# A decoder layer on one core: the last three token blocks in idle banks, chunks ahead of a down projection, and filling transposes

## The chip, the cores and the metric

The kernel runs on one core of one Trainium2 chip. The metric is the device time of one execution in microseconds (us), lower is better. TensorE, VectorE (DVE), ScalarE (ACT), GpSimd (POOL) and the DMA queue of SyncE (SP) each work through a queue of their own in order; semaphores order them against each other.

## The reference

The input `x` has 8 batches of 256 tokens with 512 features. Three residual layers follow each other, each with a layer norm behind it:

```python
x = _layernorm(x + _L0_attn_ref(x, Wi, Wf, Wg, w_norm, Wo))      # gated linear recurrence
x = _layernorm(x + _L0_xattn_ref(8, 256, 512, w, u, x, ctx_2048)) # WKV: two recurrences, a division
x = _layernorm(x + _L0_ffn_ref(x, w_gate_up, w_down))
```

The change touches the third one, a feed-forward layer with values rounded to whole multiples of a scale for each row:

```python
def _quant_dequant(v, axis):
    scale = jnp.max(jnp.abs(v), axis=axis, keepdims=True) / QMAX
    scale = jnp.maximum(scale, EPS)
    q = jnp.clip(jnp.round(v / scale), -QMAX, QMAX)
    return q * scale

xq = _ste(x, axis=-1)                      # _ste gives the value of _quant_dequant
gate_up = jnp.einsum('bsh,oh->bso', xq, _ste(w_gate_up, axis=-1))
gate, up = (gate_up[..., :I], gate_up[..., I:])        # I = 1408
h = jax.nn.silu(gate) * up
return jnp.einsum('bsi,oi->bso', _ste(h, axis=-1), _ste(w_down, axis=-1))
```

A token's hidden row of 1408 values has to be complete before its maximum, and so its scale, is known; only then can it be rounded and projected down.

## The kernel before

A batch of 256 tokens is two token blocks of 128; block `n = 2b + t` is block `t` of batch `b`, 0 to 15 in all. Each engine's program is an order written out by hand. A prologue handles the first batches and the weights; a loop over `iteration(b, par)` runs the feed-forward layer of batch `b` beside the WKV layer of batch `b + 1` and the recurrence of batch `b + 2`. Behind the loop stands a tail, again by hand: the feed-forward layer of batch 6 beside the WKV layer of batch 7 (there is no batch 8), and then the feed-forward layer of batch 7 alone. The whole change lies in the tail.

A token block goes through the feed-forward layer in these steps, named by their functions:

- `mlp_up(b, par, t, [c])`, PE: chunk `c` of the up projection. There are three chunks, of 512, 512 and 384 hidden columns; each is 8 matmuls, 4 for the gate and 4 for the up half, into one of two slots of `slot_ps` (two banks each), slot `(t + c) % 2`. PE may write a slot when VectorE or ACT has read what lay in it.
- `scale_products(b, t, [c])`, DVE: multiplies the gate half into `gate_buf` and the up half into `hid_buf(t)` by the scales of the weights' rows; the second of them frees the slot (`mlp_read`).
- `silu(b, par, t, [c])`, ACT, in place in `gate_buf`; `hidden(b, t, [c])`, POOL: the product of both, in place in `hid_buf(t)` (`hid_ready`).
- `hidden_max_row(b, t)`, DVE: the largest magnitude of the whole row. For block 15 it is taken in pieces: `hidden_max(b, t, c)` for each chunk and `hidden_max_last` over the three. `hidden_scale`, DVE: three one-column instructions to `hid_inv`.
- `round_hidden(n, t, part)`, ACT: rounds the row in two parts of 768 and 640 columns. `turn_hidden(n, t, part)`, PE: turns them by 6 and 5 transposes into a slot. `read_hidden(n, t, part)`, ACT: copies them into `hqT` (`hq_ready`).
- `mlp_down(n, t)`, PE: 11 matmuls of 512 columns into the first bank of slot `(t + 1) % 2`. `read_down`, DVE: reads and scales them into `z3` (`down_read`).
- `residual_3`, POOL, `layer_norm_3`, DVE, `rstd_3`, POOL (four one-column instructions), `normalise_3`, ACT: the residual and the layer norm; the store follows on SP. For blocks 14 and 15 VectorE does the residual and the normalising itself (`residual_last`, `layer_norm_last`, `normalise_last`), with `rstd_last` on POOL.

In the tail `turn_keys(7)`, `exponential(7)`, `divide(7)`, `refine(7)`, `turn_values(7)`, `residual_2(7)`, `round_2(7)`, `turn_inputs(7)` and `read_inputs(7)` belong to batch 7's WKV layer and to the inputs of its feed-forward layer. `turn_values(7)` waits until both halves have been refined (`y_ready`), which follows their division (`y0_ready`). ACT changes between two sets of function tables with `exp_tables` and `silu_tables`.

PSUM has eight banks: `slot_ps` four, `turn_ps` two (keys, values and inputs are turned there) and `proj_ps` two, for the projections of the first layer. Behind the loop nothing uses `proj_ps`, and behind `read_inputs(7)` nothing uses `turn_ps`. `keep_busy(count, spare)` on PE is `count` transposes of a 128x128 identity into a spare place whose result nobody reads; before the change it is called in the prologue only.

## Time and profile before

| | us |
|---|---|
| median of 3 runs | 429.62 |
| lowest, highest | 428.13, 433.3 |
| the profiled execution, its own time | 429.65 |
| its span on the core | 427.8 |

| engine | busy us | share of the span |
|---|---|---|
| PE, matmuls | 376.4 | 88% |
| DVE | 363.6 | 85% |
| ACT | 320.8 | 75% |
| POOL | 233.2 | 55% |

The span runs from the first to the last instruction that the profile shows; the time of an execution has 1.85 us around it. The mean granted clock of TensorE is 0.981 of full speed. The tail behind the loop begins at about 361 us on PE. Matmul ends are modelled, and of a group of eleven matmuls the trace sometimes holds ten.

### The profile page before, as it was taken

The page shows a single profiled execution, that of the slowest core. Times are in us where ns is not written, and L with a number is a line of the kernel's source. Part 1 is how long each engine was busy: PE and PEld are TensorE (multiplying, and loading weights), DVE is VectorE, ACT ScalarE, POOL GpSimd, SP SyncE. Part 2 cuts the span into 40 slices and gives each one's busy share as a digit, 9 for nine tenths or more (in the row PEclk, how much of TensorE's full clock was granted, in tenths as well). Part 3 has the DMA queues.
Part 4 walks back from the last instruction along what each step waited for, and adds up shares of the span by engine and source line. Part 5 has one row for each costly group of instructions (what it writes and reads, how often), then busy time and mean ns, then how long its engine had stood idle before and what let it go on. Part 6 is the DMA issues. An engine that isn't in the chain of part 4 may idle for free.

```text
span 427.8 us, 8024 instructions
## 1 busy us (share of the span) xinstructions
PE 376.4 (88%) x2820; PEld 294.0 (69%) x2842; DVE 363.6 (85%) x620; ACT 320.8 (75%) x422; POOL 233.2 (55%) x274
## 2 busy tenths in 40 slices
PE   7898889979898899999999999999999998486772
PEld 6797789867876597759775977597759774233331
DVE  3789888493999799989998999899999999997664
ACT  3688578649926799589957996799679976975761
POOL 1574555343552854766475747674667554644441
PEclk9999999999999999999999999999999999888988
DMA  7946451663020002020203020302030202000101
GB/s 250 389 150 247 106 207 40 235 52 92 2 100 1 0 2 76 10 115 0 75 2 123 3 74 2 123 0 74 0 123 0 74 0 74 26 1 0 51 25 51
DMA packets 12843, 31.75 MB, mean 74 GB/s; under 512 B 2038, under 2 KB 5132, under 8 KB 12812
## 3 DMA queue, kind: packets, MB, share of 16 engines
...
## 4 chain that ended last, share of the span: by engine, by line
DVE 26%; PE 26%; ACT 15%; issue 15%; POOL 12%; DMA 3%; SPq 2%; POOLq 0%; DVEq 0%; ACTq 0%
PE proj_ps L477 15%; PE slot_ps L580 6%; POOL den L1243 4%; DVE stats L1558 2%; POOL ring L1268 2%; ACT L983 2%; DMA den<-wiT_dram 2%; ACT hqT L948 2%; PE slot_ps L615 2%; DVE inp L1461 2%; DVE ring L1603 2%; DVE ring L1600 2%; DVE num L1551 2%; DVE x_max L1577 2%; POOL z L1273 2%
## 5 line engine op out<-in xcount | busy, mean ns | idle before, releaser
L1268 POOL TENSOR_TENSOR ring<-ring 128x512 f32<-128x512 f32 (+1 forms) x48 | 64.1, 1337 | 43.9 <-ACT ring L934 43.9
L580 PE MATMUL slot_ps<-w1q,xqT 128*128 128x512 bf16 (+1 forms) x377 | 80.2, 362 | 5.4 <-DVE ring L1603 2.4
L477 PE MATMUL proj_ps<-x_high,proj_high 128*128 128x256 f32 x384 | 64.7, 290 | 3.2 <-DVE inp L1480 2.2
L580 PEld LDWEIGHTS slot_ps<-w1q,xqT 128*128 128x128 bf16 x384 | 36.1, 98 | 44.6 <-issue 3.6
L477 PE MATMUL proj_ps<-x_low,proj_high 128*128 128x256 f32 x384 | 61.6, 282 | 0.0
L477 PE MATMUL proj_ps<-x_high,proj_low 128*128 128x256 f32 x384 | 61.6, 282 | 0.0
L477 PEld LDWEIGHTS proj_ps<-x_high,proj_high 128*128 128x128 f32 x384 | 53.2, 189 | 5.2 <-issue 3.6
L477 PEld LDWEIGHTS proj_ps<-x_high,proj_low 128*128 128x128 f32 x384 | 52.7, 188 | 0.0
L477 PEld LDWEIGHTS proj_ps<-x_low,proj_high 128*128 128x128 f32 x384 | 52.6, 188 | 0.0
L615 PE MATMUL slot_ps<-w2q,hqT 128*128 128x512 bf16 x161 | 43.8, 418 | 6.9 <-ACT hqT L948 4.7
L934 ACT ACTIVATE ring<-ring,zero_bias,x_scale 128x512 f32<-128x512 f32 (+1 forms) x48 | 36.8, 772 | 16.8 <-DVE ring L1600 16.7
L1243 POOL TENSOR_TENSOR den<-den,q_state 128x512 f32<-128x512 f32 x16 | 28.7, 1807 | 31.5 <-ACT q_state L894 31.5
L1600 DVE TENSOR_TENSOR ring<-slot_ps,scale_rows 128x512 f32<-128x512 f32 (+1 forms) x48 | 30.6, 637 | 10.5 <-PE slot_ps L580 10.1
L1204 POOL TENSOR_SCALAR ring<-ring,row_inv 128x512 f32<-128x512 f32 (+1 forms) x26 | 28.2, 1095 | 18.8 <-DVE row_inv L1695 18.8
L615 PEld LDWEIGHTS slot_ps<-w2q,hqT 128*128 128x128 bf16 x176 | 17.0, 105 | 27.6 <-issue 11.5
L941 ACT ACTIVATE ring<-ring,round_bias,hid_inv 128x768 f32<-128x768 f32 (+1 forms) x32 | 29.6, 966 | 7.1 <-DVE hid_inv L1641 7.1
L1603 DVE TENSOR_TENSOR ring<-slot_ps,scale_rows 128x512 f32<-128x512 f32 (+1 forms) x48 | 30.5, 635 | 0.0
L948 ACT ACTIVATE hqT<-slot_ps,half_bias 128x768 bf16<-128x768 f16 (+1 forms) x32 | 25.3, 836 | 4.9 <-PE slot_ps L600 4.8
L1238 POOL TENSOR_TENSOR num<-num,c_sb 128x512 f32<-128x512 f32 x16 | 20.5, 1281 | 15.2 <-ACT num L878 14.5
L1619 DVE TENSOR_REDUCE hid_top<-ring 128x1 f32<-128x1408 f32 x15 | 24.2, 1610 | 5.4 <-POOL ring L1268 5.4
L1502 DVE TENSOR_TENSOR_SCAN q_state<-decay_col,turn_ps 128x256 f32<-128x256 f32 x32 | 20.1, 671 | 4.5 <-ACT turn_ps L882 4.5
...
## 6 DMA issues: line engine op xcount, KB each, us to landing
...
```

The lines of the kernel that those rows point to most:

```text
L477: last = nc.tensor.matmul(out, a, b, start=(i == 0), stop=(i == len(terms) - 1))
L580: last = nc.tensor.matmul(slot_ps[:, s, half * 512:half * 512 + width], xqT[:, par, d, t * P:(t + 1) * P], w1q[:, d, half * I + at:half * ...
L615: last = nc.tensor.matmul(slot_ps[:, s, 0:D], hqT[:, i, :], w2q[:, i, :], start=(i == 0), stop=(i == IB - 1))
L934: nc.scalar.activation(g, g, ACT.Silu, bias=zero_bias[:, :], scale=x2_scale[:, par, t:t + 1]).then_inc(silu_ready, 1)
L941: nc.scalar.activation(h, h, ACT.Identity, bias=round_bias[:, :], scale=hid_inv[:, t:t + 1]).then_inc(hid_rounded, 1)
L948: nc.scalar.activation(hqT[:, first:first + count, :].rearrange("p i t -> p (i t)"), part_16((t + 1 + NC) % 2, part), ACT.Identity, bias=h ...
L1204: last = nc.gpsimd.tensor_scalar(rows[:, a, :], rows[:, a, :], row_inv[:, c:c + 1], ROUND, ALU.mult, ALU.add)
L1243: nc.gpsimd.tensor_tensor(blocks(den, h), blocks(den, h), blocks(rec_copy, h), ALU.mult).then_inc(newton_ready, 1)
L1268: nc.gpsimd.tensor_tensor(hid, hid, gate_buf[:, at:at + width], ALU.mult).then_inc(hid_ready, 1)
L1600: nc.vector.tensor_tensor(gate_buf[:, at:at + width], slot_ps[:, s, 0:width], scale_rows[:, at:at + width], ALU.mult).then_inc(gate_scaled, 1)
L1603: nc.vector.tensor_tensor(hid_buf(t)[:, at:at + width], slot_ps[:, s, 512:512 + width], scale_rows[:, I + at:I + at + width], ALU.mult).th ...
L1619: nc.vector.tensor_reduce(hid_top[:, :], hid_buf(t)[:, 0:I], AX.X, ALU.max, apply_absolute_value=True).then_inc(hid_top_ready, 1)
```

## The change

It has five parts, all for the tail.

1. For blocks 13, 14 and 15 (`n >= TAIL`) the hidden row is turned into `proj_ps`, and down projections go into `turn_ps`, its first bank for block 14 and its second for 13 and 15. The waits follow: a turn no longer waits for the next block's products to be read, but for `hq_ready` of the part that lay in the bank before. The up projection of block 15 waits for `mlp_read` of block 14, not for block 13's down projection.
2. PE: the three chunks of block 15 stand ahead of `mlp_down(13, 1)`.
3. DVE: the maximum of block 14 is taken in pieces too, with the products of block 15's first chunk before the third piece. `read_down(12)` moves behind the maximum and the scale of block 13, `layer_norm_3(12)` into the middle of block 14's products, `read_down(13)` and `layer_norm_3(13)` back to and behind block 15's pieces.
4. ACT: block 11 is rounded right behind the exponentials and read right behind the first SiLU block; blocks 13 to 15 get another order of SiLU, rounding, reading and `normalise_3`. POOL: `rstd_3(12)` and `residual_3(13)` move behind the products of blocks 14 and 15.
5. PE: eight calls of `keep_busy`, of 14 to 24 transposes each. Ahead of one of them stands a new wait for `y0_ready`.

```diff
@@ -29,6 +29,8 @@
 TB = T // P
 IB = I // P
 TILES = BATCHES * TB
+
+TAIL = TILES - 3
 EPS = 1e-5
 QMAX = 127.0
 QEPS = 1e-8
@@ -207,6 +209,18 @@
             return r.rearrange("p (a d) -> p a d", a=1), slice(UP_LOADS + q, UP_LOADS + q + 1)
 
         gate_buf = ring[:, 2, :]
+
+        def turned_hidden(n, t, part):
+
+            if isinstance(n, int) and n >= TAIL:
+                return proj_ps[:, part, 0:PARTS[part][1] * P // 2].bitcast(F16)
+            return part_16((t + 1 + NC) % 2, part)
+
+        def down_ps(n, t):
+
+            if isinstance(n, int) and n >= TAIL:
+                return turn_ps[:, t * 512:t * 512 + D]
+            return slot_ps[:, (t + NC) % 2, 0:D]
 
         def hid_buf(par):
             return ring[:, par, :]
@@ -570,9 +584,15 @@
                             pe.wait_ge(xq_ready, b + 1)
                         if isinstance(n, int) and n == 0:
                             pe.wait_ge(rows_kept, LOADS)
-                        wait(pe, hq_ready, 2 * n - 2)
+                        if isinstance(n, int) and n >= TAIL + 2:
+                            pe.wait_ge(mlp_read, (n - 1) * NC + 2)
+                        else:
+                            wait(pe, hq_ready, 2 * n - 2)
                     elif c == 1:
-                        wait(pe, down_read, n - 1)
+                        if isinstance(n, int) and n >= TAIL + 2:
+                            pe.wait_ge(mlp_read, n * NC)
+                        else:
+                            wait(pe, down_read, n - 1)
                     else:
                         pe.wait_ge(mlp_read, n * NC + 1)
                     for half in range(2):
@@ -590,14 +610,16 @@
 
             def turn_hidden(n, t, part):
 
-                s = (t + 1 + NC) % 2
-                if isinstance(n, int) and n == TILES - 1:
-                    pe.wait_ge(down_read, n)
                 pe.wait_ge(hid_rounded, 2 * n + part + 1)
-                pe.wait_ge(mlp_read, chunks_read(n) - 1)
+                if isinstance(n, int) and n >= TAIL:
+                    pe.wait_ge(z1_ready, TILES)
+                    if n > TAIL:
+                        pe.wait_ge(hq_ready, 2 * n + part - 1)
+                else:
+                    pe.wait_ge(mlp_read, chunks_read(n) - 1)
                 first, count = PARTS[part]
                 for i in range(count):
-                    last = nc.tensor.transpose(part_16(s, part)[:, i * P:(i + 1) * P],
+                    last = nc.tensor.transpose(turned_hidden(n, t, part)[:, i * P:(i + 1) * P],
                                                low_halves(hid_buf(t)[:, (first + i) * P:
                                                                      (first + i + 1) * P]),
                                                identity16[:, :])
@@ -605,14 +627,17 @@
 
             def mlp_down(n, t, parts=(0, 1)):
 
-                s = (t + NC) % 2
-                if parts[0] == 0:
+                if isinstance(n, int) and n >= TAIL:
+                    pe.wait_ge(xq_ready, BATCHES)
+                    if n >= TAIL + 2:
+                        pe.wait_ge(down_read, n - 1)
+                elif parts[0] == 0:
                     pe.wait_ge(mlp_read, chunks_read(n))
                 for part in parts:
                     first, count = PARTS[part]
                     pe.wait_ge(hq_ready, 2 * n + part + 1)
                     for i in range(first, first + count):
-                        last = nc.tensor.matmul(slot_ps[:, s, 0:D], hqT[:, i, :], w2q[:, i, :],
+                        last = nc.tensor.matmul(down_ps(n, t), hqT[:, i, :], w2q[:, i, :],
                                                 start=(i == 0), stop=(i == IB - 1))
                 if parts[-1] == 1:
                     last.then_inc(down_done, 1)
@@ -775,34 +800,45 @@
                 iteration(b + 1, 1)
 
 
+            spare = proj_ps[:, 0, 0:P // 2]
             mlp_up(6, 0, 0, [0])
             turn_keys(7, 0)
             turn_keys(7, 1)
             mlp_up(6, 0, 0, [1])
             mlp_up(6, 0, 0, [2])
+            pe.wait_ge(z1_ready, TILES)
+            keep_busy(16, spare)
             turn_hidden(11, 1, 0)
             turn_hidden(11, 1, 1)
+            keep_busy(24, spare)
             mlp_down(11, 1)
             mlp_up(6, 0, 1, [0])
+            keep_busy(16, spare)
+            pe.wait_ge(y0_ready, 16)
+            keep_busy(16, spare)
             turn_values(7, 0)
             turn_values(7, 1)
             mlp_up(6, 0, 1, [1])
             mlp_up(6, 0, 1, [2])
+            keep_busy(16, spare)
             turn_hidden(12, 0, 0)
             turn_hidden(12, 0, 1)
+            keep_busy(14, spare)
             mlp_down(12, 0)
             turn_inputs(7)
+            keep_busy(16, spare)
             mlp_up(7, 1, 0, [0])
             mlp_up(7, 1, 0, [1])
             mlp_up(7, 1, 0, [2])
             turn_hidden(13, 1, 0)
             turn_hidden(13, 1, 1)
-            mlp_down(13, 1)
             mlp_up(7, 1, 1, [0])
             mlp_up(7, 1, 1, [1])
             mlp_up(7, 1, 1, [2])
+            mlp_down(13, 1)
             turn_hidden(14, 0, 0)
             turn_hidden(14, 0, 1)
+            keep_busy(14, turn_ps[:, 0:P // 2])
             mlp_down(14, 0)
             turn_hidden(15, 1, 0)
             turn_hidden(15, 1, 1)
@@ -947,7 +983,7 @@
                 first, count = PARTS[part]
                 nc.scalar.activation(
                     hqT[:, first:first + count, :].rearrange("p i t -> p (i t)"),
-                    part_16((t + 1 + NC) % 2, part), ACT.Identity,
+                    turned_hidden(n, t, part), ACT.Identity,
                     bias=half_bias[:, :]).then_inc(hq_ready, 1)
 
             def keep_rows(q):
@@ -1139,15 +1175,15 @@
             exp_tables()
             exponential(7, 0)
             exponential(7, 1)
+            round_hidden(11, 1, 0)
+            round_hidden(11, 1, 1)
             silu_tables()
             silu(6, 0, 0, [0])
+            read_hidden(11, 1, 0)
+            read_hidden(11, 1, 1)
             silu(6, 0, 0, [1])
-            round_hidden(11, 1, 0)
             silu(6, 0, 0, [2])
             normalise_3(10, 0)
-            round_hidden(11, 1, 1)
-            read_hidden(11, 1, 0)
-            read_hidden(11, 1, 1)
             exp_tables()
             logarithm(7, 0)
             reciprocal(7, 0)
@@ -1169,20 +1205,20 @@
             silu(7, 1, 0, [0])
             round_hidden(13, 1, 1)
             silu(7, 1, 0, [1])
+            silu(7, 1, 0, [2])
             read_hidden(13, 1, 0)
+            read_hidden(13, 1, 1)
+            silu(7, 1, 1, [0])
             normalise_3(12, 0)
-            silu(7, 1, 0, [2])
-            read_hidden(13, 1, 1)
             round_hidden(14, 0, 0)
-            silu(7, 1, 1, [0])
             silu(7, 1, 1, [1])
             round_hidden(14, 0, 1)
             silu(7, 1, 1, [2])
             read_hidden(14, 0, 0)
             read_hidden(14, 0, 1)
-            normalise_3(13, 1)
             round_hidden(15, 1, 0)
             round_hidden(15, 1, 1)
+            normalise_3(13, 1)
             read_hidden(15, 1, 0)
             read_hidden(15, 1, 1)
 
@@ -1404,13 +1440,13 @@
             residual_3(12, 0, 0)
             rstd_3(11, 1)
             hidden(7, 0, [0])
-            rstd_3(12, 0)
             hidden(7, 0, [1])
             hidden(7, 0, [2])
-            residual_3(13, 0, 1)
+            rstd_3(12, 0)
             hidden(7, 1, [0])
             hidden(7, 1, [1])
             hidden(7, 1, [2])
+            residual_3(13, 0, 1)
             rstd_3(13, 1)
             rstd_last(14, 0)
             rstd_last(15, 1)
@@ -1590,7 +1626,10 @@
                 for c in chunks:
                     at, width = CHUNKS[c]
                     dve.wait_ge(mlp_done, n * NC + c + 1)
-                    if c == 0:
+                    if isinstance(n, int) and n == TILES - 1:
+                        dve.wait_ge(hid_ready, (n - 1) * NC + c + 1)
+                        dve.wait_ge(hq_turned, 2 * n - 2)
+                    elif c == 0:
                         if isinstance(n, int) and n == 0:
                             dve.wait_ge(scales_spread[0], 16)
                             dve.wait_ge(scales_spread[1], 16)
@@ -1607,6 +1646,8 @@
 
             def hidden_max(b, t, c):
                 n = b * TB + t
+                if c == 0 and n == TILES - 1:
+                    dve.wait_ge(hid_top_ready, n)
                 at, width = CHUNKS[c]
                 dve.wait_ge(hid_ready, n * NC + c + 1)
                 nc.vector.tensor_reduce(hid_max[:, c:c + 1], hid_buf(t)[:, at:at + width], AX.X,
@@ -1621,7 +1662,7 @@
 
             def hidden_max_last(b, t):
                 n = b * TB + t
-                dve.wait_ge(hid_max_ready, NC)
+                dve.wait_ge(hid_max_ready, (n - TILES + 3) * NC)
                 nc.vector.tensor_reduce(hid_top[:, :], hid_max[:, :], AX.X,
                                         ALU.max).then_inc(hid_top_ready, 1)
 
@@ -1648,8 +1689,7 @@
                     dve.wait_ge(scales_spread[2], 16)
                 dve.wait_ge(down_done, n + 1)
                 wait(dve, out_stored[t], b * 16)
-                s = (t + NC) % 2
-                nc.vector.scalar_tensor_tensor(z3[:, t, :], slot_ps[:, s, 0:D],
+                nc.vector.scalar_tensor_tensor(z3[:, t, :], down_ps(n, t),
                                                hid_scale[:, t:t + 1], scale_rows[:, 2 * I:],
                                                ALU.mult, ALU.mult).then_inc(down_read, 1)
 
@@ -1877,25 +1917,28 @@
             scale_products(6, 1, [2])
             scale_2(7, 1)
             layer_norm_3(11, 1)
-            read_down(12, 6, 0)
             hidden_max_row(6, 1)
             hidden_scale(6, 0, 1)
-            layer_norm_3(12, 0)
+            read_down(12, 6, 0)
             scale_products(7, 0, [0])
             scale_products(7, 0, [1])
+            layer_norm_3(12, 0)
             scale_products(7, 0, [2])
-            hidden_max_row(7, 0)
+            hidden_max(7, 0, 0)
+            hidden_max(7, 0, 1)
+            scale_products(7, 1, [0])
+            hidden_max(7, 0, 2)
+            hidden_max_last(7, 0)
             hidden_scale(7, 1, 0)
+            scale_products(7, 1, [1])
+            scale_products(7, 1, [2])
+            hidden_max(7, 1, 0)
             read_down(13, 6, 1)
-            scale_products(7, 1, [0])
-            scale_products(7, 1, [1])
-            hidden_max(7, 1, 0)
-            scale_products(7, 1, [2])
-            layer_norm_3(13, 1)
             hidden_max(7, 1, 1)
             hidden_max(7, 1, 2)
             hidden_max_last(7, 1)
             hidden_scale(7, 1, 1)
+            layer_norm_3(13, 1)
             read_down(14, 7, 0)
             residual_last(14, 0)
             layer_norm_last(14, 0)
```

## Rows read from the trace of the kernel before

**Rows 1.** Windows of the tail: busy time by engine, then TensorE's granted clock, DMA

```profile
...
core 0: us, PE busy (x) PEld busy (x) DVE busy (x) ACT busy (x) POOL busy (x), PEclk, DMA share, GB/s
...
368.00:372.00 4.00, 0.98 (x11) 0.79 (x11) 3.96 (x8) 4.00 (x6) 3.27 (x3) 0.85 0.12 44
...
372.00:376.00 4.00, 3.46 (x11) 1.31 (x10) 4.00 (x8) 3.92 (x6) 0.48 (x2) 0.50 0.07 26
...
412.00:416.00 4.00, 3.65 (x10) 1.29 (x9) 1.29 (x6) 2.73 (x4) 0.84 (x4) 0.61 0.18 66
...
```

**Rows 2.** Timeline of PE: start, duration, instruction, and the idle time before it

```profile
...
369.42 0.51 PE L600 MATMUL slot_ps<-identity,ring 128*128 128x128 f16 x6 [3.94 <-ACT ring L941]
...
372.78 4.47 PE L615 MATMUL slot_ps<-w2q,hqT 128*128 128x512 bf16 x10 [0.54 <-ACT hqT L948]
...
380.48 1.09 PE L546 MATMUL turn_ps<-identity,num 128*128 128x128 f32 x8 [1.27 <-DVE num L1545]
...
387.89 3.99 PE L615 MATMUL slot_ps<-w2q,hqT 128*128 128x512 bf16 x10 [1.23 <-DVE ring L1603]
...
393.53 5.01 PE L580 MATMUL slot_ps<-w1q,xqT 128*128 128x512 bf16 x24 [1.21 <-ACT xqT L925]
...
405.69 3.20 PE L580 MATMUL slot_ps<-w1q,xqT 128*128 128x512 bf16 x16 [0.42 <-DVE z L1652]
...
416.71 0.79 PE L600 MATMUL slot_ps<-identity,ring 128*128 128x128 f16 x11 [0.85 <-DVE z L1652]
...
418.31 2.53 PE L615 MATMUL slot_ps<-w2q,hqT 128*128 128x512 bf16 x11 [0.80 <-ACT hqT L948]
...
```

**Rows 3.** Timeline of DVE in the tail, same columns

```profile
...
377.29 0.75 DVE L1652 SCALAR_TENSOR_TENSOR z<-slot_ps,hid_scale,scale_rows 128x512 f32<-128x512 f32 x1
...
380.34 0.68 DVE L1600 TENSOR_TENSOR ring<-slot_ps,scale_rows 128x512 f32<-128x512 f32 x1
...
381.61 1.28 DVE L1551 TENSOR_TENSOR num<-x,turn_ps 128x512 f32<-128x512 f32 x2
...
391.91 0.75 DVE L1652 SCALAR_TENSOR_TENSOR z<-slot_ps,hid_scale,scale_rows 128x512 f32<-128x512 f32 x1 [1.91 <-PE slot_ps L615]
...
392.58 1.61 DVE L1619 TENSOR_REDUCE hid_top<-ring 128x1 f32<-128x1408 f32 x1
...
402.66 1.62 DVE L1619 TENSOR_REDUCE hid_top<-ring 128x1 f32<-128x1408 f32 x1 [3.06 <-POOL ring L1268]
...
404.89 0.74 DVE L1652 SCALAR_TENSOR_TENSOR z<-slot_ps,hid_scale,scale_rows 128x512 f32<-128x512 f32 x1
...
411.24 1.21 DVE L1612 TENSOR_REDUCE hid_max<-ring 128x1 f32<-128x512 f32 x2
...
412.48 0.16 DVE L1625 TENSOR_REDUCE hid_top<-hid_max 128x1 f32<-128x3 f32 x1
...
420.88 0.75 DVE L1652 SCALAR_TENSOR_TENSOR z<-slot_ps,hid_scale,scale_rows 128x512 f32<-128x512 f32 x1 [2.31 <-PE slot_ps L615]
...
```

**Rows 4.** Timeline of ACT in the tail, same columns

```profile
...
395.19 0.81 ACT L912 ACTIVATE z<-z,shift,rstd 128x512 f32<-128x512 f32 x1 [1.71 <-POOL shift L1289]
...
395.91 1.01 ACT L941 ACTIVATE ring<-ring,round_bias,hid_inv 128x768 f32<-128x768 f32 x1
...
396.82 0.80 ACT L934 ACTIVATE ring<-ring,zero_bias,x_scale 128x512 f32<-128x512 f32 x1
...
397.53 0.91 ACT L941 ACTIVATE ring<-ring,round_bias,hid_inv 128x640 f32<-128x640 f32 x1
...
417.26 1.58 ACT L948 ACTIVATE hqT<-slot_ps,half_bias 128x768 bf16<-128x768 f16 x2 [1.70 <-PE slot_ps L600]
...
```

**Rows 5.** Timeline of POOL in the tail, same columns

```profile
...
388.78 2.22 POOL L1268 TENSOR_TENSOR ring<-ring 128x512 f32<-128x512 f32 x2 [3.16 <-ACT ring L934]
...
392.75 1.27 POOL L1273 TENSOR_TENSOR z<-z,x 128x512 f32<-128x512 f32 x1 [1.74 <-DVE z L1652]
...
```

**Rows 6.** Timeline of PE: filling transposes of the head, same columns

```profile
...
70.16 5.98 PE L657 MATMUL slot_ps<-identity 128*128 128x128 f16 x104
...
```

## The prediction

> **What bounds the kernel now.** I read the windows of the tail first, then the timelines of the four engines beside the chain that ended last, and followed the chain in the queues. The edits all begin after the loop, where batch 7's last layers and token blocks 11 to 15 run, so 361 us of the span are untouched.
>
> Three things are to be seen. First, from 366 to 389 us VectorE has no gap: in 368 to 376 it is busy 7.96 of 8 us [rows 1]. Its `read_down(11)` at 377.29 has no idle time before it, nor do the products at 380.34 and `residual_2` at 381.61 [rows 3]. Second, TensorE waits often and three times runs at half rate. It had nothing for 3.94 us before the turn at 369.42 [rows 2]; the granted clock averaged 0.85 in 368 to 372 and was 0.50 in 372 to 376, the 1.2 GHz level, and 0.61 in 412 to 416 [rows 1]. At that level ten recorded matmuls of `mlp_down(11)` take 4.47 us and ten of `mlp_down(12)` 3.99; at full rate eleven of `mlp_down(15)` take 2.53 [rows 2]. Third, from 389 us blocks 13, 14 and 15 follow each other by latency: POOL's hidden product, VectorE's maximum (1.62 us for the whole row, after 3.06 us of idling at 402.66), scale, ACT's rounding, turn, read, down projection. VectorE waited 2.31 us for the last one at 420.88 [rows 3].
>
> **The change part by part**, as a walk through the queues after 361 us, each instruction starting when its engine and its releasers are free. Durations are start-to-start: on ACT a `round_hidden` part 0.91, a SiLU block 0.71, part 1 0.81 (its 0.91 less the 0.1 by which neighbours overlap) [rows 4]; a pair of products 1.2 and a read-out 0.67 on VectorE [rows 3]; a 512-column product on POOL 1.27, both blocks of 388.78 together 2.22, so the 384-column one 0.95 [rows 5]; an up chunk 1.7 and 1.3 at full rate (3.20 for the last two with the pipeline's end) [rows 2].
>
> *Blocks 11 and 12, to 389 us: no gain.* ACT's instructions to `exp_tables` are the same ones in another order and ACT was never idle there, so it gets to the logarithm at the same time. Rounding block 11 right behind the exponentials brings its turn to 366.5, its read-out to 370.3, and `mlp_down(11)` ends near 372.7 in place of 377.25. Its reader, VectorE, is free only at 377.29 [rows 3]: the 4.5 us go into slack. The three SiLU blocks that pay for it are some 1.8 us later; but VectorE takes their maximum only 2.2 us ahead of its read-out at 377.29, at 375.1 [rows 3], a us after POOL is done. `keep_busy` costs 104 transposes per 5.98 us, 0.057 each [rows 6]: 16 are 0.9 us, 24 are 1.4, and all but one group lie in time in which TensorE waits. Cover gone, each costs those 0.9 us.
>
> *The one that doesn't* stands behind the new wait on `y0_ready`. Down projection 11 and the first up chunk of block 13 end at 374.5, a filler at 375.4; then TensorE has nothing until `divide(7,1)` ends at 379.2. That is 3.8 us, as long as the 3.94 us after which the clock fell in the trace [rows 1, 2]. Behind the wait stand 16 more transposes, then `turn_values`, due at 380.48 [rows 2]. At full rate they end at 380.1 and cost nothing. At half rate they end at 381.0 and the eight fp32 turns after them (1.09 us at full rate) may take up to 0.9 more, before `residual_2`, which stood at 381.61 on an engine without slack. Bounds 0 and 1.3 us; I take 0.6, since the rows speak for a fall while the fillers themselves help the clock back. The Trainium skill has this in "TensorE: Matmul & The Clock Gate", section "HAM oscillation — how this bites in real kernels": long waits between bursts of matmuls make each burst start at the slow rate. By it the sum would carry the upper part of that bound.
>
> *Down projection 12* starts where it did, at 387.9 (it waits for block 13's last product), and at full rate ends 1.6 us sooner. Batch 7's inputs are turned behind it, now when ACT's rounding ends (390.7, not 391.7), so the up projection of block 14 starts at 392.6, not at 393.53 [rows 2].
>
> *`read_down(12)` behind the maximum.* Block 13's hidden row is complete on POOL at 391.0 [rows 5]. Maximum and scale take 2.23 us (402.66 to 404.89) [rows 3], so its scale is ready at 393.3, 1.5 us sooner. But `read_down(12)` moves from 391.91 to 393.3, and with it goes POOL's `residual_3(12)`, which stood at 392.75 [rows 5]; behind it on POOL is `rstd_3(11)`, and ACT's `normalise_3(11)`, which stood at 395.19 after 1.71 us of waiting for just that [rows 4], moves by the same 1.35 to 396.5. Behind it on ACT are `round_hidden(13)` and all SiLU blocks of block 14. So the earlier scale is not used, and the rounding starts 1.3 us late (397.3, was 395.91).
>
> *Block 14* gets this back. ACT: rounding and SiLU alternating to 401.0, `read_hidden(13)` to 402.5. POOL multiplies block 14 at 399.05, 400.6 and 401.8 and is done at 402.8, as before. The maximum by pieces (two in 1.21 us [rows 3]) leaves only 0.5 us and the 0.2 us of the combination behind the last product, where the whole row took 1.62; but a pair of block 15's products (1.2 us) stands before the last piece. Scale 14 comes at 405.0, was 404.9.
>
> *Block 15's chunks ahead of down projection 13.* Turned hidden rows lie in the idle `proj_ps`, down results in `turn_ps`, so chunks 0 to 2 of block 15 run from 400.2 to 405.3 and no longer wait for `read_down(13)`, as the one at 405.69 did [rows 2]. Down projection 13 follows to 407.6, at a time when nobody needs it. VectorE multiplies block 15 at 402.5, 405.0 and 406.2. ACT: SiLU at 403.2, `normalise_3(12)` to 404.7, rounding 14 from 405.1, the other two SiLU blocks at 406.0 and 407.55. POOL ends the last product at 409.3, the last piece follows at 409.35, and the scale of block 15 is there at 410.7. Before, the pieces from 411.24 and the combination at 412.48 [rows 3] put it at 413.3: 2.6 us gained, the main term.
>
> *The end.* ACT rounds block 15 at 410.8 to 412.5. `normalise_3(13)` then waits for POOL: `residual_3(13)` now follows the last product (409.3 to 410.6), statistics behind the scale to 411.6, and the `rstd_3` chain about 1.2 us, so it runs at 412.85 to 413.6. `read_hidden(15)` stands behind it and starts at 413.6, was 417.26 [rows 4]. From there the code is as before: 3.62 us from that start to VectorE's last `read_down` (417.26 to 420.88), then 6.9 us to the end of the span. Had `normalise_3` no place there, another us would be gained.
>
> Sum: 413.6 − 417.26 = −3.7; with the 0.6 of the half-rate fillers −3.1. The profiled execution took 429.65 us, its span 427.8 and 1.85 around it: 429.65 − 3.1 = 426.5. It stands 0.03 us above the median of three, 429.62, so nothing is to be corrected, but these three lay 5.2 us apart. About 2% (8.6 us) is what a measurement of this kernel can tell from no change.
>
> **The rivals.**
>
> *A. More is gained.* The move of `read_down(12)` doesn't delay ACT, because the stretch to 389 us ends earlier than I think or the waits on it are not ACT's last. For it speaks that ACT's 1.71 us of waiting came from a projection that the change speeds up; against it, that POOL takes the residual first in its queue. Price 1.35 us, and no half-rate fillers, 0.6: 424.5.
>
> *B. Transposes don't hold the clock.* Then the new fillers do nothing and half rate stays where it was. In the head the clock stayed full over 104 of them [rows 6], which speaks against it. Down projection 11 has 2.3 us of slack left; 12 at half rate ends at 391.9, before its new reader at 393.3. Down projection 14 at half rate ends at 413.7 instead of 411.6 and holds the turn of block 15 behind it, so that its read-out starts at 414.3: 0.7 us. 427.2.
>
> *C. The last projection loses the clock.* TensorE has only eleven short turns from 411.5, the end of down projection 14, to 414.4. That is 2.9 us, where the like gap before 418.31 was 2.4 and kept the full clock [rows 2]; the one of 3.94 us before 369.42 lost it; this one lies between. Eleven matmuls at half rate cost 2.0 to 2.3: 428.7.
>
> *D. Slower: TensorE waits in long stretches and restarts at half rate each time.* Its queue is emptied sooner, so the gaps at 375.4 (1.3 us), at 397.5 to 400.2 (the up chunks of block 15, on which VectorE then waits: 1.6 us) and at 411.5 (2.3 us) each start a slow burst: −3.7 + 5.2 = +1.5, so 431.1. It decides from the point where two of the three are slow and the third is the last. Against it: the fillers and, in the middle gap, the turns of block 13.
>
> **How the numbers follow.** The forecast 0.45, between 425.9 (no slow fillers) and 427.2 (their full price). A 0.15, B 0.12, C 0.18, D 0.10. B lies inside the forecast's range. The range reaches over A and C and 1 us beyond them for the spread of runs: 423.4 to 429.7, and leaves out D. Faster by over 2% would need 421.0, three us beyond A: 0.03. Slower by over 2% needs 438.2, seven beyond D: 0.01. Within 2%: 0.96.
>
> **What would show it.** In the profile of the changed kernel: `read_down(11)` still at about 377.3; the fillers behind `divide` at 0.107 or 0.057 us each; `normalise_3(11)` near 396.5, released by POOL; the scales of blocks 14 and 15 near 405.0 and 410.7; `normalise_3(13)` before `read_hidden(15)` waiting for POOL; the last `read_down` near 417.2. The forecast is wrong if VectorE's run from 366 to 389 is longer, which moves everything, if ACT isn't delayed at 395 (A), or if the granted clock is 0.5 in the last 3 us of matmuls (C, D).

## The result, and the profile after

The change makes the kernel slower. Before: 429.26 us, after: 431.89 us (medians of 20 runs each); the ratio is 1.0059, with a 95% interval of 1.0041 to 1.0076. That is 2.6 us more where 3.1 less were forecast; the time lies outside the range of 423.4 to 429.7 and inside the 2% to which the prediction gave 0.96. The ratios, here and below, leave out two executions that stand far above the others of their kernel, one of e5_pool_beside_scans (436.17 us) and one of e10_best_again (762.41 us), while the medians hold them. The profiled execution has a span of 430.7 us, where before had 427.8.

Executions differ already ahead of the tail, so stretches of the tail are compared from a landmark: the start of ACT's `normalise_1(7)`, which the change doesn't move. First this row in the timeline of ACT before, then the same row after, with the rows of ACT after that answer to [rows 4]:

```profile
...
359.78 1.52 ACT L906 ACTIVATE x<-inp,shift,rstd 128x512 f32<-128x512 f32 x2 [1.12 <-POOL shift L1232]
...
```

```profile
...
359.02 1.52 ACT L942 ACTIVATE x<-inp,shift,rstd 128x512 f32<-128x512 f32 x2 [1.12 <-POOL shift L1268]
...
389.79 1.59 ACT L984 ACTIVATE hqT<-slot_ps,half_bias 128x768 bf16<-128x768 f16 x2 [4.78 <-PE slot_ps L622]
...
399.90 0.81 ACT L948 ACTIVATE z<-z,shift,rstd 128x512 f32<-128x512 f32 x1 [4.00 <-POOL shift L1325]
...
418.02 0.81 ACT L948 ACTIVATE z<-z,shift,rstd 128x512 f32<-128x512 f32 x1 [0.80 <-POOL shift L1325]
418.74 1.56 ACT L984 ACTIVATE hqT<-proj_ps,half_bias 128x768 bf16<-128x768 f16 x2
...
```

From the landmark to the end of the span are 427.8 − 359.78 = 68.0 us before and 430.7 − 359.02 = 71.7 after. These are two single executions, and a tail can be long in one of them. The landmark lies between 359.0 and 362.4 us in the 14 profiles of this document, at 360.8 in the mean, though nothing that was changed stands ahead of it; before and after have early ones. An estimate for a typical tail is the median time less the 1.85 us around the span and less 360.8: 66.6 us before, 69.3 after. By that the two profiled tails are 1.4 and 2.4 us longer than typical. Which instruction waits for which is read from the profiles below; what a change is worth is read from the timed runs.

VectorE after, where [rows 3] are before:

```profile
...
369.86 4.31 DVE L1556 TENSOR_TENSOR_SCAN p_state<-decay_col,num 128x256 f32<-128x256 f32 x4
374.09 2.47 DVE L1564 SCALAR_TENSOR_TENSOR num<-num,bonus_col,p_state 128x255 f32<-128x255 f32 x4
...
378.70 0.74 DVE L1692 SCALAR_TENSOR_TENSOR z<-slot_ps,hid_scale,scale_rows 128x512 f32<-128x512 f32 x1
...
384.33 1.28 DVE L1587 TENSOR_TENSOR num<-x,turn_ps 128x512 f32<-128x512 f32 x2 [1.31 <-PE turn_ps L560]
...
394.41 1.62 DVE L1660 TENSOR_REDUCE hid_top<-ring 128x1 f32<-128x1408 f32 x1 [1.60 <-POOL ring L1304]
...
396.64 0.74 DVE L1692 SCALAR_TENSOR_TENSOR z<-slot_ps,hid_scale,scale_rows 128x512 f32<-128x512 f32 x1
...
406.98 0.69 DVE L1639 TENSOR_TENSOR ring<-slot_ps,scale_rows 128x512 f32<-128x512 f32 x1 [1.07 <-PE slot_ps L600]
...
409.53 0.68 DVE L1639 TENSOR_TENSOR ring<-slot_ps,scale_rows 128x512 f32<-128x512 f32 x1
...
417.25 0.69 DVE L1705 TENSOR_TENSOR z<-z,x 128x512 f32<-128x512 f32 x1
...
423.76 0.75 DVE L1692 SCALAR_TENSOR_TENSOR z<-turn_ps,hid_scale,scale_rows 128x512 f32<-128x512 f32 x1 [4.63 <-PE turn_ps L640]
...
```

The two rows at the top are what the prediction didn't have. The four scans of `sum_values` and the four numerators take 6.8 us in all. Before they took 4.6. One line of the program at a time, scans and numerators before and then the same after (the shortest, median and longest of one instruction, in ns; the four in the window of the tail):

```profile
...
L1520 DVE TENSOR_TENSOR_SCAN p_state<-decay_col,num x4: 659/660/1207, 370.6 to 372.9; 128x256 f32<-128x256 f32 x4
...
```

```profile
...
L1528 DVE SCALAR_TENSOR_TENSOR num<-num,bonus_col,p_state x4: 454/474/474, 373.5 to 374.7; 128x255 f32<-128x255 f32 x4
...
```

```profile
...
L1556 DVE TENSOR_TENSOR_SCAN p_state<-decay_col,num x4: 660/1090/1701, 369.9 to 372.8; 128x256 f32<-128x256 f32 x4
...
```

```profile
...
L1564 DVE SCALAR_TENSOR_TENSOR num<-num,bonus_col,p_state x4: 453/472/1309, 374.1 to 375.2; 128x255 f32<-128x255 f32 x4
...
```

The shortest are the same. Single ones are held up: a scan of 0.66 us takes 1.70, a numerator of 0.47 takes 1.31. POOL's timeline shows what ran beside them. Before, the three hidden products of block 12 ended at 371.27, during the first of the four scans:

```profile
...
367.81 3.46 POOL L1268 TENSOR_TENSOR ring<-ring 128x512 f32<-128x512 f32 x3 [0.43 <-ACT ring L934]
...
```

After, they run until 373.61, and `newton(7, 0)` follows at 375.00:

```profile
...
368.80 1.27 POOL L1304 TENSOR_TENSOR ring<-ring 128x512 f32<-128x512 f32 x1 [2.17 <-ACT ring L970]
370.97 2.64 POOL L1304 TENSOR_TENSOR ring<-ring 128x512 f32<-128x512 f32 x2 [0.90 <-ACT ring L970]
...
375.00 1.28 POOL L1279 TENSOR_TENSOR den<-den,q_state 128x512 f32<-128x512 f32 x1 [0.40 <-ACT q_state L930]
...
417.29 0.70 POOL L1325 TENSOR_TENSOR shift<-neg_mean,rstd 128x1 f32<-128x1 f32 x1
...
```

TensorE after, where [rows 2] are before, and the granted clock in windows of 1 us (PE busy, clock, DMA share, GB/s):

```profile
...
369.87 2.32 PE L640 MATMUL slot_ps<-w2q,hqT 128*128 128x512 bf16 x10 [1.42 <-ACT hqT L984]
...
373.75 1.06 PE L682 MATMUL proj_ps<-identity 128*128 128x128 f16 x16
380.70 1.89 PE L682 MATMUL proj_ps<-identity 128*128 128x128 f16 x16 [5.89 <-DVE turn_ps L1573]
382.38 1.91 PE L560 MATMUL turn_ps<-identity,num 128*128 128x128 f32 x8
384.51 4.01 PE L600 MATMUL slot_ps<-w1q,xqT 128*128 128x512 bf16 x15 [0.22 <-issue]
...
403.49 6.60 PE L600 MATMUL slot_ps<-w1q,xqT 128*128 128x512 bf16 x24
...
413.89 2.53 PE L640 MATMUL turn_ps<-w2q,hqT 128*128 128x512 bf16 x11
...
419.98 3.73 PE L640 MATMUL turn_ps<-w2q,hqT 128*128 128x512 bf16 x10 [2.25 <-ACT hqT L984]
...
```

```profile
...
378.00:379.00 1.00, 0.00 (x0) 1.00 0.00 0
...
380.00:381.00 1.00, 0.30 (x4) 0.50 0.00 0
...
385.00:386.00 1.00, 1.00 (x4) 0.50 0.00 0
...
388.00:389.00 1.00, 1.00 (x16) 1.00 0.00 0
...
404.00:405.00 1.00, 1.00 (x3) 0.50 0.00 0
...
421.00:422.00 1.00, 1.00 (x4) 0.50 0.00 0
...
```

Down projection 11 ends early as forecast (369.87, ten recorded matmuls in 2.32 us, was 4.47). Then TensorE waits 5.89 us for `divide`, and by 380 the granted clock is 0.50, the 1.2 GHz level: the 16 transposes behind the wait take 1.89 us, the turns behind them 1.91, and the second up chunk of block 13 runs slow until the clock is back at 387 (seven matmuls of it, and the third chunk at full rate, in 4.01 us). It happens twice more: in the up chunks of block 15 (6.60 us for 24, where 24 before took 5.01), and in the last down projection (3.73 for ten recorded, was 2.53 for eleven).

From the landmark, in us; "walk" is the prediction's walk without its 0.6 for slow fillers:

| | before | walk | after | e1_act_order |
|---|---|---|---|---|
| `read_down(11)` starts | 17.5 | 17.5 | 19.7 | 17.6 |
| `residual_2(7)` | 21.8 | 21.8 | 25.3 | 22.0 |
| maximum of block 13 | 32.8 | 31.3 | 35.4 | 31.4 |
| `read_down(12)` | 32.1 | 33.5 | 37.6 | 33.7 |
| `normalise_3(11)` | 35.4 | 36.7 | 40.9 | 36.9 |
| scale of block 14 ready | 45.1 | 45.2 | 50.5 | 45.4 |
| scale of block 15 ready | 53.5 | 50.9 | 56.2 | 51.1 |
| `read_hidden(15)` | 57.5 | 53.8 | 59.7 | 54.5 |
| last `read_down` | 61.1 | 57.4 | 64.7 | 59.6 |
| end of the span | 68.0 | 64.3 | 71.7 | 66.5 |

### The profile page after: what moved, and what is told of

The parts are those of the page before. It is cut to its first block, busy times and chain, and to the rows that moved or that the text cites. A ratio compares the mean times of both kernels' runs of the same rounds, so it can differ in the third digit from the quotient of the medians.

```text
span 430.7 us, 8292 instructions
## 1 busy us (share of the span) xinstructions
PE 384.0 (89%) x2950; PEld 303.8 (71%) x2974; DVE 367.2 (85%) x623; ACT 320.3 (74%) x422; POOL 233.6 (54%) x274
## 4 chain that ended last, share of the span: by engine, by line
DVE 28%; PE 26%; issue 14%; ACT 14%; POOL 12%; DMA 3%; SPq 1%; POOLq 0%; DVEq 0%; ACTq 0%
PE proj_ps L491 15%; PE slot_ps L600 7%; POOL den L1279 4%; DVE stats L1594 2%; DMA den<-wiT_dram 2%; DVE inp L1497 2%; POOL ring L1304 2%; ACT hqT L984 2%; POOL z L1309 2%; ACT L1019 2%; DVE ring L1642 2%; DVE ring L1639 2%; DVE num L1587 2%; DVE x_max L1613 2%; DVE p_state L1556 1%
## 5 line engine op out<-in xcount | busy, mean ns | idle before, releaser
L1304 POOL TENSOR_TENSOR ring<-ring 128x512 f32<-128x512 f32 (+1 forms) x48 | 64.5, 1345 | 51.1 <-ACT ring L970 51.0
L600 PE MATMUL slot_ps<-w1q,xqT 128*128 128x512 bf16 (+1 forms) x375 | 82.2, 370 | 4.4 <-DVE ring L1642 2.4
L491 PE MATMUL proj_ps<-x_high,proj_high 128*128 128x256 f32 x384 | 64.7, 290 | 2.1 <-DVE inp L1516 2.0
L970 ACT ACTIVATE ring<-ring,zero_bias,x_scale 128x512 f32<-128x512 f32 (+1 forms) x48 | 36.7, 771 | 19.2 <-DVE ring L1639 19.2
L1240 POOL TENSOR_SCALAR ring<-ring,row_inv 128x512 f32<-128x512 f32 (+1 forms) x26 | 27.2, 1059 | 19.3 <-DVE row_inv L1735 19.3
L640 PE MATMUL slot_ps<-w2q,hqT 128*128 128x512 bf16 x130 | 31.0, 379 | 2.9 <-ACT hqT L984 2.0
L1660 DVE TENSOR_REDUCE hid_top<-ring 128x1 f32<-128x1408 f32 x14 | 22.5, 1610 | 4.0 <-POOL ring L1304 4.0
L640 PEld LDWEIGHTS slot_ps<-w2q,hqT 128*128 128x128 bf16 x143 | 12.8, 98 | 16.3 <-issue 3.4
L984 ACT ACTIVATE hqT<-slot_ps,half_bias 128x768 bf16<-128x768 f16 (+1 forms) x26 | 20.4, 836 | 5.1 <-PE slot_ps L622 5.1
```

The lines of the kernel that those rows point to most:

```text
L491: last = nc.tensor.matmul(out, a, b, start=(i == 0), stop=(i == len(terms) - 1))
L600: last = nc.tensor.matmul(slot_ps[:, s, half * 512:half * 512 + width], xqT[:, par, d, t * P:(t + 1) * P], w1q[:, d, half * I + at:half * ...
L640: last = nc.tensor.matmul(down_ps(n, t), hqT[:, i, :], w2q[:, i, :], start=(i == 0), stop=(i == IB - 1))
L970: nc.scalar.activation(g, g, ACT.Silu, bias=zero_bias[:, :], scale=x2_scale[:, par, t:t + 1]).then_inc(silu_ready, 1)
L984: nc.scalar.activation(hqT[:, first:first + count, :].rearrange("p i t -> p (i t)"), turned_hidden(n, t, part), ACT.Identity, bias=half_bi ...
L1240: last = nc.gpsimd.tensor_scalar(rows[:, a, :], rows[:, a, :], row_inv[:, c:c + 1], ROUND, ALU.mult, ALU.add)
```

## The experiments

The last column above is the first experiment. Twelve runs were made (e10 is e7 again), in three groups, each group on one chip. Ratios are to the kernel before on the same chip; the tail is measured from the landmark to the end of the span in the one profiled execution.

| run | median us | ratio (95%) | tail us |
|---|---|---|---|
| before | 429.26 | 1 | 68.0 |
| after | 431.89 | 1.0059 (1.0041 to 1.0076) | 71.7 |
| e1_act_order | 429.32 | 1.0013 (0.9977 to 1.0050) | 66.5 |
| e2_no_y0_fill | 431.57 | 1.0066 (1.0035 to 1.0097) | 71.2 |
| e3_before_act_only | 432.45 | 1.0071 (1.0043 to 1.0098) | 69.9 |
| e4_no_fill | 431.52 | 1.0049 (1.0016 to 1.0082) | 67.7 |
| e5_pool_beside_scans | 433.21 | 1.0061 (1.0018 to 1.0103) | 70.1 |
| e6_read_down_first | 427.00 | 0.9955 (0.9926 to 0.9985) | 64.2 |
| e7_normalise_last | 424.34 | 0.9887 (0.9820 to 0.9954) | 62.1 |
| e8_fill_before_last | 424.64 | 0.9888 (0.9824 to 0.9952) | 63.5 |
| e9_best_no_fill | 424.83 | 0.9899 (0.9866 to 0.9931) | 63.0 |
| e10_best_again | 425.66 | 0.9913 (0.9881 to 0.9945) | 62.4 |
| e11_new_act_order | 428.36 | 0.9992 (0.9971 to 1.0013) | 65.6 |
| e12_statistics_later | 425.49 | 0.9922 (0.9897 to 0.9948) | 62.2 |

### ACT's old order in the changed kernel

Theory 1: ACT's new order of blocks 11 and 12 moves POOL's products of block 12 onto VectorE's scans, and these stop each other. Theory 2: the loss is all TensorE's, by slow bursts and fillers.

```diff
 exponential(7, 1)
-round_hidden(11, 1, 0)
-round_hidden(11, 1, 1)
 silu_tables()
 silu(6, 0, 0, [0])
-read_hidden(11, 1, 0)
-read_hidden(11, 1, 1)
 silu(6, 0, 0, [1])
+round_hidden(11, 1, 0)
 silu(6, 0, 0, [2])
 normalise_3(10, 0)
+round_hidden(11, 1, 1)
+read_hidden(11, 1, 0)
+read_hidden(11, 1, 1)
```

> The changed kernel with ACT's old order of blocks 11 and 12 (SiLU blocks before the roundings). Theory 1 (POOL's products of block 12 now run beside VectorE's scans and numerators, which read two SBUF operands, and stop them): the four scans fall back from 4.31 to about 2.95 us and the four numerators from 2.47 to 1.64, block 12's maximum comes 2.2 us sooner and the kernel gains at least those 2.2 us over the changed one, so about 429.5 or less. Theory 2 (the loss is TensorE's: slow bursts and fillers): the scans stay as long as they are and the time moves by less than 1 us.

The scans over PSUM, those over SBUF and the numerators on VectorE, and POOL's three products of block 12, which now end before the scans have gone far:

```profile
...
370.05 1.25 DVE L1538 TENSOR_TENSOR_SCAN q_state<-decay_col,turn_ps 128x256 f32<-128x256 f32 x2
...
372.13 2.97 DVE L1556 TENSOR_TENSOR_SCAN p_state<-decay_col,num 128x256 f32<-128x256 f32 x4
375.03 1.64 DVE L1564 SCALAR_TENSOR_TENSOR num<-num,bonus_col,p_state 128x255 f32<-128x255 f32 x4
...
```

```profile
...
369.34 3.46 POOL L1304 TENSOR_TENSOR ring<-ring 128x512 f32<-128x512 f32 x3 [0.43 <-ACT ring L970]
...
```

They are back at 2.97 and 1.64 us, and `read_down(11)` is at 17.6 us from the landmark. The ratio falls from 1.0059 to 1.0013, which is 2.0 us, back to the time of before. In the profiled execution the tail is 1.5 us shorter than before, and its steps follow the prediction's walk within 0.2 us up to the scale of block 15. What is missing at the end is 0.6 at `normalise_3(13)` and 1.6 more by the last down projection, at half rate:

```profile
...
416.99 3.84 PE L640 MATMUL turn_ps<-w2q,hqT 128*128 128x512 bf16 x10 [2.09 <-ACT hqT L984]
...
```

Theory 1 holds; theory 2 alone falls. But the timed runs don't show the 1.5 us that the profiled tail gains over before: by them e1 is 0.6 us slower than before (between 1.0 faster and 2.1 slower), where −3.1 was forecast. So the collision isn't the whole miss.

### The wait on `y0_ready` and its fillers

```diff
 keep_busy(16, spare)
-pe.wait_ge(y0_ready, 16)
-keep_busy(16, spare)
 turn_values(7, 0)
```

> The changed kernel without the wait on y0_ready and the 16 transposes behind it. If the transposes at half rate hold up the turn of the values, turn_values starts at the end of refine and the time falls by 0.5 to 1.3 us. If instead the half rate behind them is what costs, the turns start 0.5 us sooner but the clock comes back later or not at all, and the time stays within 0.5 us or rises.

`residual_2` comes 0.44 us sooner (24.87 from the landmark, was 25.31), and the time doesn't move (1.0066, where 1.0059 was without the edit). The transposes that stand in the way cost about what the prediction's first half of that term said (0.5); the other half, the slow turns, stays: `turn_values` takes 1.96 us where it took 1.09 before. So the slow burst isn't made by the fillers: it comes behind the wait for VectorE (7.07 us in this run) with none of them behind it.

### The kernel before with the new ACT order alone

```diff
 exponential(7, 1)
+round_hidden(11, 1, 0)
+round_hidden(11, 1, 1)
 silu_tables()
 silu(6, 0, 0, [0])
+read_hidden(11, 1, 0)
+read_hidden(11, 1, 1)
 silu(6, 0, 0, [1])
-round_hidden(11, 1, 0)
 silu(6, 0, 0, [2])
 normalise_3(10, 0)
-round_hidden(11, 1, 1)
-read_hidden(11, 1, 0)
-read_hidden(11, 1, 1)
```

> The kernel before with the new ACT order of blocks 11 and 12 alone. Theory 1: scans and numerators get 2.2 us longer in all, and with no slack on VectorE until 389 us the kernel is about 2.2 us slower (431.5). Theory 2: the order by itself does nothing, within 0.5 us of before.

```profile
...
372.49 4.29 DVE L1520 TENSOR_TENSOR_SCAN p_state<-decay_col,num 128x256 f32<-128x256 f32 x4
376.70 2.47 DVE L1528 SCALAR_TENSOR_TENSOR num<-num,bonus_col,p_state 128x255 f32<-128x255 f32 x4
...
```

```profile
...
384.49 1.81 PE L546 MATMUL turn_ps<-identity,num 128*128 128x128 f32 x8 [5.20 <-DVE num L1545]
...
```

4.29 and 2.47 us, 2.2 more than before, with none of the other edits. The kernel is slower by 0.71% (3.0 us, between 1.8 and 4.2), where 2.2 was expected. Beside the collision, TensorE, done with block 11 sooner than before, waits 5.20 us for the values and turns them at half rate (1.81 us, was 1.09); against it, down projection 12 runs at full rate in this profile (2.32 us for ten, was 3.99), and the profiled tail is only 1.9 us longer than before. This part alone costs as much in the timed runs as the whole change does.

### No fillers in the tail

From the changed kernel, and so for all eight groups:

```diff
-keep_busy(16, spare)
-pe.wait_ge(y0_ready, 16)
-keep_busy(16, spare)
 turn_values(7, 0)
...
-keep_busy(14, turn_ps[:, 0:P // 2])
 mlp_down(14, 0)
```

> The changed kernel without any of the eight groups of filling transposes and without the wait on y0_ready. If the fillers that stand between up projection and turn of block 12 cost time and hold no clock that matters, this is 0.5 to 2 us faster than the changed kernel. If they hold the clock for down projections 11, 12 and 14, this is 1 us or more slower than it.

The time stays (1.0049 against 1.0059, intervals overlap). Half rate comes in other places: down projection 11 takes 4.47 us and block 14's up chunks 6.61, but in this execution the last down projection runs at full rate. The profiled tail is 4.0 us shorter than after (67.7 and 71.7), but the medians are 0.4 us apart: this is how far a profiled tail can stand from the timed runs. The fillers change where the clock falls; a change of the time is not shown, and one of 1.6 us would lie inside the two intervals.

### Two POOL products beside the scans

```diff
 hidden(6, 0, [2])
+pool.wait_ge(z1_ready, TILES)
+for spare_out in (forget, gate):
+    nc.gpsimd.tensor_tensor(flat_half(spare_out, 0), flat_half(forget, 1),
+                            flat_half(forget, 1), ALU.mult).then_inc(spare_done, 1)
 first_token(7)
```

> The kernel before, with two extra POOL products of 512 columns (two SBUF operands, results in buffers that nobody reads any more) behind block 12's products, so that they run in POOL's idle time beside VectorE's last scans. ACT and TensorE are untouched. Theory 1 (a POOL product stops a VectorE instruction with two SBUF operands for as long as it runs): scans and numerators together take 1 to 2.5 us longer than 4.6 us, and the kernel is slower by about as much (430 to 431.5 in place of 429). Rival (the scans of the changed kernel were slow for another reason, such as ACT's order): scans and numerators stay at 4.6 us and the time within 0.5.

```profile
...
373.25 4.55 DVE L1525 TENSOR_TENSOR_SCAN p_state<-decay_col,num 128x256 f32<-128x256 f32 x4
377.73 2.47 DVE L1533 SCALAR_TENSOR_TENSOR num<-num,bonus_col,p_state 128x255 f32<-128x255 f32 x4
...
```

```profile
...
373.88 1.42 POOL L1399 TENSOR_TENSOR forget<-forget 128x512 f32<-128x512 f32 x1
375.26 1.42 POOL L1399 TENSOR_TENSOR gate<-forget 128x512 f32<-128x512 f32 x1
...
```

In the kernel before, with the code of ACT and TensorE untouched, the products stretch the scans to 4.55 us; pushed back, the numerators then meet `newton` and take 2.47. Together 2.4 us more, and the kernel is 0.61% slower (2.6 us; the interval is wide: of the nine executions behind it three took 429.4 to 430.0 us and six 431.7 to 434.7, and the profile is of a long one, with block 14's up chunks slow too). This is the suspected cost, made by itself. The Trainium skill says in "SBUF — State Buffer", section "SBUF: two separate sides", that VectorE and GpSimd share a pair of ports that one of them holds for a whole instruction while the other stops, and that a VectorE instruction with two SBUF inputs comes under this when the GpSimd instruction reads SBUF. By that rule, a scan whose operand comes from PSUM runs on beside a product, as the two scans of `sum_weights` at 370.05 do beside POOL's products from 369.34 in the profile of e1_act_order (0.6 us each), and one whose operands both lie in SBUF doesn't. The traces agree: after, the product that starts at 370.97 ends at 372.28, and the scan that started at 371.13 ends 0.55 us behind it. They agree also the other way: after, POOL's `shift` at 417.29 takes 0.70 us in place of 0.19 beside VectorE's two-operand residual at 417.25.

### `read_down(12)` first again

On top of e1_act_order:

```diff
 layer_norm_3(11, 1)
+read_down(12, 6, 0)
 hidden_max_row(6, 1)
 hidden_scale(6, 0, 1)
-read_down(12, 6, 0)
```

> The changed kernel with ACT's old order of blocks 11 and 12 (as in the run of that name) and with read_down(12) ahead of block 13's maximum again. By the prediction's step the move of read_down(12) delays POOL's residual and ACT's normalise_3(11): that run had ACT idle for 4.0 us before it, at 398.2. Expected: normalise_3(11) some 2.9 us sooner against batch 7's first-layer landmark, the maximum no later, and 2 to 2.9 us less than that run, about 427. Rival: block 14 is paced by VectorE and TensorE, and under 0.7 us comes through.

`normalise_3(11)` in e1_act_order, and then with this edit:

```profile
...
398.22 0.81 ACT L948 ACTIVATE z<-z,shift,rstd 128x512 f32<-128x512 f32 x1 [4.00 <-POOL shift L1325]
...
```

```profile
...
395.51 0.82 ACT L948 ACTIVATE z<-z,shift,rstd 128x512 f32<-128x512 f32 x1 [0.97 <-POOL shift L1325]
...
```

ACT's wait for POOL falls from 4.00 to 0.97 us, `normalise_3(11)` comes at 33.9 from the landmark (was 36.9), and the time is 427.0, for the first time clearly below before (ratio 0.9955, 2.5 us less than that of e1). The profiled tail is 2.3 us shorter. The delay that the prediction put down to this move is real.

### `normalise_3(13)` behind the reads of block 15

On top of e6_read_down_first:

```diff
-normalise_3(13, 1)
 read_hidden(15, 1, 0)
 read_hidden(15, 1, 1)
+normalise_3(13, 1)
```

> The same, with normalise_3(13) behind both reads of block 15 on ACT. The prediction put 1 us on ACT's wait for POOL's shift there. Expected: the last read starts where the turned row is there, 1 to 1.6 us sooner than with the order of the changed kernel. Rival: the down projection's clock takes it back.

```profile
...
411.56 1.56 ACT L984 ACTIVATE hqT<-proj_ps,half_bias 128x768 bf16<-128x768 f16 x2
...
```

```profile
...
412.79 2.32 PE L640 MATMUL turn_ps<-w2q,hqT 128*128 128x512 bf16 x10 [0.64 <-ACT hqT L984]
...
```

The last read starts 50.8 us from the landmark, 1.6 sooner than in the run before it (52.4), and TensorE's wait shrinks to 0.64 us, behind which the clock stays full (2.32 us for ten). 424.34 us, ratio 0.9887.

The move has a price of its own, which bounds what it gives. Blocks 13 and 15 share a buffer of `z3`, so the last `read_down` may write only when block 13 has been stored, and that store now comes late. It is issued at 413.85 and lands 2.0 us later; the down projection is done at 415.11, and VectorE waits 0.8 us more:

```profile
...
415.94 0.75 DVE L1692 SCALAR_TENSOR_TENSOR z<-turn_ps,hid_scale,scale_rows 128x512 f32<-128x512 f32 x1 [2.56 <-DMA out_dram<-z]
...
```

It is so in e9, e10, e11 and e12 too. No run gives block 15 another buffer.

The same kernel as e7 once more:

> The kernel of the run e7_normalise_last once more, with more rounds: old ACT order of blocks 11 and 12, read_down(12) first, normalise_3(13) last. Expected: 1.0 to 1.3% faster than before (424 to 425), as there.

425.66 us, or 425.20 without the execution of 762.41; ratio 0.9913 (0.9881 to 0.9945): 0.9% faster than before, a little under the 1.0 expected.

### Fillers: before the last projection, and none at all

On top of e7_normalise_last:

```diff
 turn_hidden(15, 1, 1)
+pe.wait_ge(mlp_read, TILES * NC)
+keep_busy(24)
 mlp_down(15, 1)
```

> The same, with 24 filling transposes between the turn of block 15 and its down projection, where TensorE waited 2.1 to 2.25 us for ACT and then ran at half rate in two of three profiles. If fillers hold the clock there, the last eleven matmuls take 2.5 us and 0 to 1.3 us are gained; if they stand in the way (the reads come sooner than before), up to 0.7 us are lost.

424.64 us, no difference that four executions each can show (both intervals reach 0.7% to either side). In the profile the fillers end after the read is done, so the down projection starts 2.0 us behind the read's start, not 1.2. But these 0.8 us aren't lost: they lie under the wait for block 13's store, and the last `read_down` comes 4.4 us behind the read's start in both profiles. The tail is 1.4 us longer than that of e7, all of it ahead of the scale of block 15; it begins with down projection 11, at 3.47 us for ten where the same code took 2.32 in e7.

And e7_normalise_last with all `keep_busy` groups of the tail and the wait on `y0_ready` removed, as in e4_no_fill:

> The same without any filling transposes in the tail and without the wait on y0_ready. If the granted clock of the tail is worth something once the queues are right, this is 1 to 3 us slower than with them (a half-rate down projection costs 2 us where it is waited for). If the clock falls only into slack, within 0.5 us.

424.83 us, ratio 0.9899 (0.9866 to 0.9931), as good as with them as far as the intervals tell. The down projections of blocks 11, 12 and 15 on TensorE in that run:

```profile
...
372.90 4.85 PE L640 MATMUL slot_ps<-w2q,hqT 128*128 128x512 bf16 x11 [0.16 <-ACT hqT L975]
...
388.14 4.18 PE L640 MATMUL slot_ps<-w2q,hqT 128*128 128x512 bf16 x11 [0.98 <-DVE ring L1633]
...
412.99 2.54 PE L640 MATMUL turn_ps<-w2q,hqT 128*128 128x512 bf16 x11 [0.42 <-ACT hqT L975]
...
```

Down projections 11 and 12 run at half rate (4.85 and 4.18 us for eleven); the last three run at full rate without help. For 11 that costs nothing, since VectorE is busy until it has been computed. For 12 it does cost something in the profile, because VectorE now waits 1.85 us for it where it waited 0.22 in e7, and batch 7's inputs are turned behind it:

```profile
...
392.36 0.75 DVE L1683 SCALAR_TENSOR_TENSOR z<-slot_ps,hid_scale,scale_rows 128x512 f32<-128x512 f32 x1 [1.85 <-PE slot_ps L640]
...
```

The up projection of block 14 starts 33.7 us from the landmark, in e7 at 32.8 and in e10 at 33.1, and the tail is 63.0 us long where those have 62.1 and 62.4. These 0.6 to 0.9 us are too few for the timed runs to show.

### The new ACT order in the best version

The kernel of e7_normalise_last with ACT's order of blocks 11 and 12 as in the change (the first diff of this section undone).

> The changed kernel with its new ACT order of blocks 11 and 12 kept, but with read_down(12) first and normalise_3(13) last. It tells whether the collision of POOL with VectorE alone still costs its time: 2.2 us of stopped scans and numerators plus the slow burst behind the long wait, so 2.5 to 3.5 us over the version with the old order (about 427.5), near the kernel before.

428.36, ratio 0.9992, and the tail 3.2 us longer than with the old order (65.6 against 62.4). By the ratios of the timed runs (0.9992 and 0.9913) it is 3.4 us, inside the 2.5 to 3.5 expected. All of the gain of the other parts goes into it.

### `layer_norm_3(12)` behind the products

On top of e7_normalise_last:

```diff
-layer_norm_3(12, 0)
 scale_products(7, 0, [2])
+layer_norm_3(12, 0)
```

> The best version with layer_norm_3(12) behind block 14's third pair of products, not ahead of it: ACT waited 1.11 us there for VectorE. Expected 0.3 to 0.9 us less; the rival is that block 14's maximum waits for block 15's first products anyway, and nothing moves.

425.49 us, ratio 0.9922 (0.9897 to 0.9948): no change that can be measured (tail 62.2 against 62.4). ACT's wait falls from 1.11 to 0.35 us, and it waits 0.93 us more for block 15's first products. In the profile the rival is right; the timed runs alone couldn't tell it from the 0.3 us.

## Why the prediction was wrong

**The step that failed** is "Blocks 11 and 12, to 389 us: no gain", and in it the sentence that the three SiLU blocks are some 1.8 us later and that this lies in slack, because VectorE takes their maximum only at 375.1. That looked for who waits for POOL's products, and found that nobody does. It didn't look at what VectorE does while they run. They moved from VectorE's scans over PSUM to its scans and numerators over SBUF, and 2.2 us came onto an engine that the prediction itself had called without slack (e1, e3, e5, e11). In the timed runs the step is worth 2.0 us (e1 against after) to 3.4 (e11 against e10), out of the 5.7 between forecast and result. The trace of before had a sign of it: one of four scans of `sum_values` took 1.21 us and the others 0.66.

**The walk behind it holds in the profile.** Without the collision, e1 follows it within 0.2 us from `residual_2` to the scale of block 15. Its sum doesn't hold in the timed runs: e1 stands 3.7 us above the forecast by the ratios. The profile of e1 shows 2.2 of that at the end of the tail; the rest isn't placed, and part of it may be that the profiled tail of before, from which the walk starts, was a long one (68.0 us, 66.6 estimated as typical). *The main term*, block 15's scale 2.6 us sooner by chunks ahead, idle banks and pieces, measured 2.4 (53.5 to 51.1). *`read_down(12)`* behind the maximum: its delay of ACT was forecast as 1.35 us against before, and measured 1.5 in e1; undone it gave more, 3.0 us at ACT and 2.3 in the tail, because down projection 12 had become faster. *`normalise_3(13)`* in front of the last read was put at 1 us; 1.6 measured (e6 and e7), partly since POOL's `shift` ahead of it takes 0.54 us and not 0.19 there, beside VectorE's residual.

**The clock was under-priced.** For the slow burst behind the wait on `y0_ready` I took 0.6 out of bounds of 0 and 1.3; after the collision had made the wait longer (5.89 us and not 3.8) it was 1.3, the upper end: `residual_2` is 3.5 us late, 2.2 by the collision. In e1, without the long wait, it was 0.2. Then 0.6 came in front of the turn of block 12, which waited behind a slow up chunk and the fillers, 1.2 by block 15's slow up chunks and 1.4 by the last down projection. These are rival D's three places; it priced them at 1.3, 1.6 and 2.3 and gave 431.1 where 431.9 was measured. That the number is close is luck: D had no collision in it, and its three places cost 3.9 us and not 5.2. I gave it 0.10, counting on the fillers and, in the middle gap, on the turns of block 13. Its mechanism was there, but in two of the three places only behind the collision: in e1 the fillers and the turns behind `divide` and the up chunks of block 15 are back at full rate.

The third place is rival C, the last projection that loses the clock, and it stays without the collision: ten of its matmuls take 3.84 us in e1 and 3.46 in e6. C reckoned a gap of 2.9 us in front of it; from the end of down projection 14 it is 3.56 us in e1. Its 428.7 is near the 429.3 of e1, but not by its price, which was 2.0 to 2.3 where the profiles show 1.4 to 1.6. The loss ends with `normalise_3(13)` moved (e7); what bounds the last `read_down` from there on is block 13's store. In the profile, from the walk's 57.4 for the last `read_down` to the 64.7 measured, the terms are 2.2, 1.3, 0.6, 1.2, 0.6 (ACT's wait for POOL's stretched `shift`, among others) and 1.4.

*Fillers* were priced at nothing except behind the new wait, and e4, e8 and e9 find nothing lost or gained by them in the whole tail that the timed runs can tell, which is about 2 us in e4 and e9 and more in e8. What they are worth in a single place stays open, since the clock falls at other moments in other executions, and a profile shows one.
